# A projection behind attention as two float32r matmuls on split operands, with another order of the first loads and of all steps

## The reference

```
mod = silu(c) @ wmod                      # six rows of 256 per batch: sa, ca, ga, sb, cb, gb
ga, gb = sign * max(|.|, 0.25)
h = layernorm(x) * (1 + ca) + sa
q, k, v = h @ Wq + bq, h @ Wk + bk, h @ Wv + bv      # 16 query heads, 4 key/value heads, 16 wide
q, k = rope(q), rope(k)
att = softmax(causal(q k^T / 4));  y = att v          # per group of 4 query heads, then (B, T, 64)
x = x + ga * (y @ Wo + bo)                            # the projection: 64 -> 256
h = layernorm(x) * (1 + cb) + sb
x = x + gb * ffn(h)       # routed: h + (rmsnorm(h) wv + bv) wo, then a gated block 256 -> 704 -> 256
```

## Time and profile before

| | |
|---|---|
| median of 3 runs | 486.77 us |
| the profiled execution | 489.17 us |
| its span (first to last instruction) | 487.4 us |
| TensorE (PE) busy | 444.7 us |
| VectorE (DVE) busy | 338.9 us |
| ScalarE (ACT) busy | 281.7 us |
| GpSimd (POOL) busy | 225.8 us |
| mean granted TensorE clock | 0.983 of full speed |

### The profile page before, as it was taken

One profiled execution on the slowest core, in us unless ns is written; L12 is line 12 of the kernel. 1 busy time (PEld: TensorE's weight loads), 2 busy tenths in 40 slices (PEclk: granted clock), 3 DMA queues, 4 the chain that ended last, 5 costly groups with the idle time before them and its releaser, 6 DMA issues.

```text
span 487.4 us, 9404 instructions
## 1 busy us (share of the span) xinstructions
PE 444.7 (91%) x3320; PEld 372.3 (76%) x3320; DVE 338.9 (70%) x745; ACT 281.7 (58%) x574; POOL 225.8 (46%) x297
## 2 busy tenths in 40 slices
PE   2687699979999999899999999989999999999994
PEld 2275355677678589778766999879889779999994
DVE  3569968488988337998873688898687635376552
ACT  1183657676559757345487763526857488454440
POOL 5382946621283421331747506275261744348244
PEclk9997989998999999999999999999999999999998
DMA  7904020000000000020020100010001001001011
GB/s 201 300 1 137 2 88 1 1 2 5 3 1 24 1 1 2 1 86 8 3 88 1 34 2 1 5 44 3 1 33 48 1 1 45 1 2 45 1 43 44
DMA packets 16448, 16.04 MB, mean 33 GB/s; under 512 B 4105, under 2 KB 14798, under 8 KB 16402
## 3 DMA queue, kind: packets, MB, share of 16 engines
q1 hardware_dynamic: 16402, 15.43, 10.0%
HBM read 11.09 MB, written 4.21 MB: 31 GB/s over the span
## 4 chain that ended last, share of the span: by engine, by line
PE 80%; DVE 6%; ACT 5%; issue 3%; DMA 2%; SPq 2%; POOL 1%; POOLq 0%; ACTq 0%; DVEq 0%
PE banks L784 8%; PE banks L785 8%; PE banks L786 8%; PE banks L701 8%; PE banks L713 7%; PE banks L675 7%; PE banks L574 5%; PE banks L654 5%; PE banks L575 5%; PE banks L576 5%; PE banks L738 3%; PE banks L664 2%; DMA wm_st<-in_L_wmod 2%; DVE stk L1124 2%; ACT QKT L890 2%
## 5 line engine op out<-in xcount | busy, mean ns | idle before, releaser
L784 PE MATMUL banks<-gTh,guhi 128*128 128x256 f32 x352 | 101.7, 289 | 1.6 <-DVE mx L1139 1.5
L785 PE MATMUL banks<-gTl,guhi 128*128 128x256 f32 x352 | 98.1, 279 | 0.0
L786 PE MATMUL banks<-gTh,gulo 128*128 128x256 f32 x352 | 98.1, 279 | 0.0
L910 ACT ACTIVATE PT<-banks 128x1024 f32<-128x1024 f32 (+3 forms) x96 | 74.4, 809 | 29.0 <-PE banks L701 24.2
L1139 DVE TENSOR_REDUCE mxp<-banks 128x2 f32<-128x1024 f32 (+3 forms) x56 | 62.2, 1142 | 12.1 <-PE banks L675 6.7
L784 PEld LDWEIGHTS banks<-gTh,guhi 128*128 128x128 f32 x352 | 66.5, 189 | 4.2 <-issue 3.5
L785 PEld LDWEIGHTS banks<-gTl,guhi 128*128 128x128 f32 x352 | 66.4, 189 | 0.5
L786 PEld LDWEIGHTS banks<-gTh,gulo 128*128 128x128 f32 x352 | 66.4, 189 | 0.0
L675 PE MATMUL banks<-QKT 128*128 128x512 f32 (+3 forms) x192 | 53.4, 384 | 13.3 <-ACT QKT L890 5.0
L701 PE MATMUL banks<-QKT 128*128 128x512 f32 (+3 forms) x192 | 52.2, 374 | 3.0 <-DMA QKT<-mrT 1.9
L537 POOL TENSOR_SCALAR_AFFINE_SELECT PT<-PT 128x512 f32<-128x512 f32 x32 | 20.7, 647 | 67.6 <-ACT PT L910 67.6
(11 more groups left out here) (165 smaller groups left out, 1069.8 us busy)
## 6 DMA issues: line engine op xcount, KB each, us to landing
xres<-in_L_attn_x SPq DMA_DIRECT2D x8, 512.0 KB, 5.0
out_x<-xres SPq DMA_DIRECT2D x8, 512.0 KB, 3.0
wm_st<-in_L_wmod SPq DMA_DIRECT2D x1, 1024.0 KB, 8.1
modB<-mod_scratch SPq DMA_DIRECT2D x4, 256.0 KB, 3.1
wg_st<-in_L_ffn_w_gate SPq DMA_DIRECT2D x1, 704.0 KB, 5.4
wu_st<-in_L_ffn_w_up SPq DMA_DIRECT2D x1, 704.0 KB, 6.5
xres<-in_L_ffn_w_down SPq DMA_DIRECT2D x1, 640.0 KB, 5.9
wm_st<-in_L_wmod SPq DMA_DIRECT2D x1, 512.0 KB, 4.6
```

Of the source, the lines that this page charges most:

```text
L784: pe.matmul(out_, guhi[:, k, blk, :], gh, start=(m == 0 and k == 0), stop=False)
L785: pe.matmul(out_, guhi[:, k, blk, :], gl, start=False, stop=False)
L786: i = pe.matmul(out_, gulo[:, k, blk, :], gh, start=False, stop=(m == len(blocks) - 1 and k == KB - 1))
L910: act.activation(PT[:, u % 2, 2 * q:2 * q + 2, 0:CH - q0], both("prob", b, n)[:, :, 0:CH - q0], ACT.Exp, scale=float(D) ** -0.5).then_inc( ...
```

## The change

It has three parts.

1. The projection. ytm is now 128 columns wide: a rounded copy of y in the first 64 and the rest (y minus the copy) in the other 64. ynT transposes it to 128 rows; ynev evicts it twice, all 128 rows to yTs and the first 64 to yTo, whose further rows (up to 97) hold ones. A new ScalarE step, woh, rounds Wo_b twice into Wo_h (rows 0 to 63 and 64 to 127) and the bias row once; a new VectorE step, wol, writes the low part of the weight and of the bias into Wo_l. wo is then two float32r matmuls per 128 tokens: yTs by Wo_h (high and low y by the high weight) and yTo by Wo_l (high y by the low weight, and the bias). Wo_raw, Wo_b and mrT share one tile, wo_mr.
2. The first loads. The first half-megabyte of wmod is issued behind the tokens and the weights Wq, Wk and Wv, and not ahead of them. The biases get a semaphore and steps of their own (setb, asetb), so setw and asetw wait for three loads and not for six.
3. ORDER is written anew, with ten more words (setb, asetb, and four each of woh and wol).

```diff
-ACT_STEPS = dict(xev=NJ, sthi=NC, ...
+ACT_STEPS = dict(woh=1, xev=NJ, sthi=NC, ...
-DVE_STEPS = dict(wts=1, wob=1, biasq=1, ...
+DVE_STEPS = dict(wts=1, wob=1, wol=1, biasq=1, ...
 ORDER = """
-ldx ldx pzero stats rstd1 setw stats pmodc pmod vmodc norm1 norm1 rstd1 norm1 asetw vkeys wts xT4 norm1 xT5 pprep0 xev
+ldx ldx pzero stats rstd1 norm1 setw asetw pmodc vmodc wts bias6 norm1 xT4 asetb xev qkv4 setb biasq stats norm1 norm1
...
-        Wo_raw = sb("Wo_raw", [H * D + 1, C])
+        wo_mr = sb("wo_mr", [P, 2, C])
+        Wo_raw, Wo_b = wo_mr[0:H * D + 1, 0, :], wo_mr[0:H * D + 1, 1, :]
+        mrT = wo_mr[P - 32:P - 32 + 2 * H].rearrange("p a c -> p (a c)")
-        Wo_b = sb("Wo_b", [H * D + 1, C])
+        Wo_h = sb("Wo_h", [2 * H * D, C], F32R)
+        Wo_l = sb("Wo_l", [WB, C], F32R)
-        ytm = sb("ytm", [P, TPC, H * D + 1])
-        yT65 = sb("yT65", [H * D + 1, TPC, P])
+        ytm = sb("ytm", [P, TPC, 2 * H * D])
+        yTs = sb("yTs", [2 * H * D, TPC, P], F32R)
+        yTo = sb("yTo", [WB, TPC, P], F32R)
...
-            sp.dma_start(wm_st[:, :, 0:CH], wmod[:, 0:CH].rearrange("(k p) n -> p k n", p=P)).then_inc(l_modc, 16)
             load_x(0, 0)
             sp.dma_start(wq_st[:], Wq.rearrange("(k p) n -> p k n", p=P)).then_inc(l_qkv, 16)
             sp.dma_start(wk_st[:], Wk.rearrange("(k p) n -> p k n", p=P)).then_inc(l_qkv, 16)
             sp.dma_start(wv_st[:], Wv.rearrange("(k p) n -> p k n", p=P)).then_inc(l_qkv, 16)
-            sp.dma_start(bb_st[:, 0:C], bq.partition_broadcast(P)).then_inc(l_qkv, 16)
...
+            sp.dma_start(wm_st[:, :, 0:CH], wmod[:, 0:CH].rearrange("(k p) n -> p k n", p=P)).then_inc(l_modc, 16)
+            sp.dma_start(bb_st[:, 0:C], bq.partition_broadcast(P)).then_inc(l_bias, 16)
...
                 if kind == "ldW":
                     if b > 0:
-                        wait("wo", 0)
+                        wait("wol", 0)
...
                 elif kind == "wo":
                     if n == 0:
-                        wait("wob", 1)
+                        wait("wol", 1)
                     wait("ynev", n * 2 // TPC + 1)
...
                     for t in range(2):
-                        i = pe.matmul(o[:, t * C:(t + 1) * C], yT65[:, (2 * n + t) % TPC, :], Wo_b[:], start=(t == 0),
-                                      stop=(t == 1))
+                        at = (2 * n + t) % TPC
+                        pe.matmul(o[:, t * C:(t + 1) * C], yTs[:, at, :], Wo_h[:], start=(t == 0), stop=False)
+                        i = pe.matmul(o[:, t * C:(t + 1) * C], yTo[:, at, :], Wo_l[:], start=False, stop=(t == 1))
...
+                elif kind == "woh":
+                    wait("wob", 1)
+                    earlier("wo", NJ)
+                    act.activation(Wo_h[0:H * D], Wo_b[0:H * D], ACT.Copy)
+                    act.activation(Wo_h[H * D:2 * H * D], Wo_b[0:H * D], ACT.Copy)
+                    act.activation(Wo_l[WB - 1:WB], Wo_b[H * D:H * D + 1], ACT.Copy).then_inc(S["woh"], 1)
...
-                    act.activation(yT65[:].rearrange("p t n -> p (t n)"),
-                                   of("ynT", b, n)[0:H * D + 1, :], ACT.Copy).then_inc(S["ynev"], 1)
+                    o = of("ynT", b, n)
+                    act.activation(yTs[:].rearrange("p t n -> p (t n)"), o, ACT.Copy)
+                    act.activation(yTo[0:H * D].rearrange("p t n -> p (t n)"), o[0:H * D, :], ACT.Copy
+                                   ).then_inc(S["ynev"], 1)
...
+                elif kind == "wol":
+                    wait("woh", 1)
+                    dve.tensor_tensor(Wo_l[0:H * D], Wo_b[0:H * D], Wo_h[0:H * D].bitcast(F32), ALU.subtract)
+                    dve.tensor_tensor(Wo_l[H * D:H * D + 1], Wo_b[H * D:H * D + 1], Wo_l[WB - 1:WB].bitcast(F32),
+                                      ALU.subtract).then_inc(S["wol"], 1)
...
-                    dve.tensor_tensor(ytm[:, :, 0:H * D].rearrange("p t (h d) -> p t h d", h=H), o[:, :, :, 0:D],
-                                      rc[:].unsqueeze(3).to_broadcast([P, TPC, H, D]), ALU.mult
-                                      ).then_inc(S["ytm"], 1)
+                    hi, y = ytm[:, :, 0:H * D], ytm[:, :, H * D:2 * H * D]
+                    then(dve.tensor_tensor(y.rearrange("p t (h d) -> p t h d", h=H), o[:, :, :, 0:D],
+                                           rc[:].unsqueeze(3).to_broadcast([P, TPC, H, D]), ALU.mult))
+                    then(dve.tensor_copy(hi.bitcast(F32R), y))
+                    dve.tensor_tensor(y, y, hi, ALU.subtract).then_inc(S["ytm"], 1)
```

More of the change, by code:

```diff
@@ L160 @@
-h2lo fft sil ffhi fin a7 up6 a0 rs1 fflo fft ffl route route up1 up4 gate5 gate7 gate0 up6 sil ffhi ms2 fflo fft ms2
-rs2 sil fft down1 sum h2 h2 h2T7 down4 h2hi h2lo sum gate7 gate1 gate4 up5 up3 sil sil ffhi ffhi fflo fft fin ffl ffhi
-sil fflo fft down2 ffhi fft ffhi fflo sum up3 sil fft ffhi fflo down2 ffl down3 down4 sum sum sum fin fin store store
-store
+ldx ldx pzero stats rstd1 norm1 setw asetw pmodc vmodc wts bias6 norm1 xT4 asetb xev qkv4 setb biasq stats norm1 norm1
+xT5 xev qkv5 rstd1 norm1 qkvb qkvb vkeys norm1 xT7 pmod pprep0 norm1 norm1 xT6 xev qkv7 amod afwv pprep1 gmod xev qkv3
@@ new lines @@
+wts up5 sil qkvb qkvb rope gate3 fft ffl fft sthi qkvb stlo qkvb ffhi sil ffhi gate7 h2T5 fflo up4 yT6 h2hi h2lo norm2
+fflo fft sil stack2 up5 stack0 stk max2 up4 ffhi stk fft ytm max6 mxr hT5 hhi ynT2 ynev down0 down1 hmod rs1 ms1 ffhi
+max2 rope mxr sthi hlo max6 gate5 sil sum sum max0 mxr stlo mxr stack2 stk max6 max2 fin wo5 mxr mxr ffl fft mxr max6
+max0 max2 mxr mxr max6 max0 up4 fflo mneg mxr mxr ffhi fflo x1 mtT2 mrow gate3 sil fft stack6 rs1 stk down3 mxr sum
+max4 gate2 max6 sil rstd2 up3 max0 ffhi ffl store mrd mxr wo4 woh ldx mxr mxr max6 mxr fft x1 prob0 max6 mxr prob2 exp
@@ new lines @@
+up2 mxr ms1 rs1 max0 gate5 sil mxr route mxr ms2 ffhi rstd2 max6 mxr a3 hhi route fft stack0 stk hlo fflo ms2 up7 up3
+max0 mxr max4 mxr gate6 sil wo2 ffhi woh gate0 x1 fft max4 rs2 h2 ffhi sil h2 down6 down7 fflo mxr fft h2T1 h2hi ffhi
+sum max4 stack2 a6 sum norm2 fflo mxr ffl down7 h2lo mneg fin route ldG down0 max4 sum sum stk a3 max0 hmod hT2 ms2
+mtT7 mxr route mrow mrd store ms2 ms1 rs2 gate5 max6 sil rstd2 up3 max4 mxr mxr h2 h2 gate6 h2T7 h2hi max0 fft mxr
+norm2 ffhi hhi h2lo hlo prob4 up3 gate7 gate2 sil fft fin rs1 ffhi sil hmod ms1 mxr wol sil rs1 ffl exp up3 fflo fft
```

158 lines of the change are left out of this document (79 added, 79 removed).

## The result

The changed kernel took 485.09 us (median, 482.81 to 487.75), the kernel before 487.69 us on the same chip (484.96 to 490.08): ratio 0.9944, 95% interval [0.9928, 0.996]. It is 0.56% faster, some 2.7 us, where 1.6% was forecast. The sign was right and the size wrong: 0.9944 of the 486.77 us of the prediction is 484.0 us, 4.9 above the forecast and beyond its own range of 476 to 482 (the wider range, 472.5 to 485.5, takes in the rivals and holds it). The profiled run took 484.3 us.

A forecast was written before the change was run, and what follows sets the result against it. TensorE was taken to bound the kernel behind 64 us, a chain of loads, vector work and maxima ahead of it. 489.17 - 5.8 - 2.5 + 0.6 = 481.5 us profiled, median 479.1; own range 476 to 482, wider 472.5 to 485.5.

The forecast's parts named there:

- The projection's passes: Projection on TensorE: 64 float32 passes of 0.216 us become float32r at 0.113; 5.8 us less, bounds 3.3 to 6.6.
- The added work elsewhere: Added VectorE and ScalarE instructions for splits, copies and evictions, mostly hidden behind TensorE: +0.6 us, bounds 0 and +10.1.
- The head: Ahead of 64 us: new loads' order and earlier copy of the maxima rows; -2.5 us, bounds 0 and -4.5.
- The copy of the maxima rows: Head, ScalarE: mrow moves ahead of two weight pieces and the down weight, so the first prob gains 1.5 us.
- The loads' order: Head: first half-megabyte of modulation weight goes behind tokens and three projection weights; 1.0 us gained.
- the landing and the 23.6 us behind it: Head: modulation weight in at 8.9 us; first stack starts 23.6 us later, at 32.5 to 34.3 us.
- The rest of the order: Nearly every engine's row changes place; taken as worth nothing, since order does not tell how long it waits.
- the limit of 13.8 us: TensorE's empty time between 64 and 480 us, the most that an order can win there.
- Order gives back: Rival: the 5.8 us turn into new waits where VectorE is nearly full; 484 us, chance 0.16.
- Better packing: Rival: the order also closes part of TensorE's 13.8 us of gaps, say 6 us more; 473 us, chance 0.14.
- The weight load rules: Rival: each float32r pass is held to its 0.189 us weight load, 1.7 us instead of 5.8; 483 us, chance 0.04.
- Slower by VectorE: Rival: 24 added VectorE instructions are paid, with blocks by GpSimd; 488.6 up to 504, value 490 us, chance 0.11.

The follow-up runs named there:

- the run in the old order: Kernel before, its loads and order kept, with the new projection alone put in, the weight's split right behind its product with the modulation: ratio 1.0244, 12 us slower.
- the mark: The changed kernel once more, unaltered, run beside three kernels with shifted operand places: ratio 0.994 [0.9923, 0.9957] to the kernel before.

## Why the prediction was right in sign and wrong in size

*The projection's passes* (5.8 us forecast, 4.5 measured, give or take 1.6). The mechanism was right: 64 float32r records for 64 float32 passes, and the size is within the noise. The distance of starts was mis-sized, 0.120 us where 0.113 was taken from the down product of the earlier trace rows, which is 0.4 us in all. The operands' distance does not explain it: it was 64 in the earlier trace rows and is 64 here, and 192 in its place left 0.120 as it was. Why the projection's starts lie 0.120 us apart stays open. The Trainium skill (Perfetto Trace Analysis, "Identifying the Most-Contended Engine") judges TensorE's headroom by the share of peak arithmetic and by the weight loads' busy share. The rival drawn from the second, that nothing is won where no load goes away, was not borne out: 64 loads remain (6.1 us on each line), and the passes won 4.5 us.

*Nothing else on TensorE changes its speed.* This was never written as a step, it was assumed in the sum, and **it is the largest miss**: the earlier trace rows was read as a property of float32r. It is one of float32r and two addresses. Moving the feed-forward operands from distance 192 to 160 (gate, up) and from 64 to 96 (down) cost 2.3 us (0.994 against 0.9892, give or take 1.4; 2.0 us between the two runs on one chip). The trace of after showed it as 281 ns in the place of 279 on an untouched line, and as a busy sum that fell by 2.7 us instead of 6 or more.

*The added work elsewhere* (0.6 forecast, 2.3 measured, give or take 2.3; bounds 0 to 10.1). The rows are as sized: VectorE rose by 12.0 us, 10 forecast, ScalarE by 10.1, 9 forecast. The step that failed, as far as the noise lets it be told, is taking the low end "because TensorE, not VectorE, ends the waits": in the chain VectorE's share went from 6% to 11%, and the new projection brought 2.4 us of idle time in the profiles. That the new order hides most of the added work fits all runs. How much of it the matmuls ahead of the projection hide is not shown, since the run in the old order lost much of its time at the split of the weight, which the forecast priced at 0.1 us.

*The head* (2.5 forecast). The copy of the maxima rows: 1.5 forecast, 1.8 by itself. The loads' order: the landing and the 23.6 us behind it came out to within 0.3 us. Both are partly luck. The landing lies anywhere from 8.4 to 10.2 us in the ten profiles, and in the sum behind it two errors cancel: the first qkv took 2.90 us where 1.5 was put down and the bias product 1.65 instead of 0.7, while pmod took 3.60 instead of 5.85. The stack did start 2.0 us earlier than before, and yet the sign of the term was wrong, since I compared it with the old program and not with the new program and the old loads; in the new order of work the early weight is used at once, and the new place costs 1.5 to 2.2 us. That the first prob came 4 us earlier than forecast shows in little: most of the head's empty time came back between 64 and 130 us.

*The rest of the order* (0 forecast). Order and loads with the old projection are worth 3.1 us; less the copy's 1.8 and with the loads' 1.5 to 2.2 taken out, some 3 us are the rest of the order, good to no better than 2 us. Nothing in the profile before told these 3 us, and the limit of 13.8 us holds.

With measured terms: -4.5 (passes) + 2.3 (added work) + 2.3 (distance) - 3.1 (order and loads) = -3.0 us. This is no check. The added work is itself the passes less the ratio of two other runs, and in the sum every run but the mark cancels, so it returns the mark's own 0.994, 2.9 us. What the terms do show is where the 5.0 us between forecast and measurement lie: 1.3 in the passes, 2.3 in the addresses, 1.7 in the added work, and 0.6 the other way in order and loads, each good to between 1.2 and 2.3 us.

*The rivals.* "Order gives back" had the right size of time and the wrong cause: the order gave, and the addresses, the added work and the loads took. "Better packing" came by some 3 us of its 6. "The weight load rules" named 483 us, but its sign, a distance of 0.19 us, did not come. "Slower by VectorE" did not come either; the run in the old order shows VectorE as the one that TensorE waits for, though there it is VectorE that waits for ScalarE.

## What to carry to other kernels

When a change adds or resizes a tile in SBUF, compare the mean duration and the distance of starts of matmuls that it did not touch: float32r products can change speed by some per cent with the distance between their operands' addresses, and a few unused bytes put that right. Look at where each new step stands in the row of its engine: a split whose second half waits for another engine cost VectorE 6.2 us of waits in one order and none in the other. Test order and arithmetic apart, since here each of them alone tells a different story (12 us slower, 0.6% faster). A load moved back in the queue is free only if nothing in the new program could have used it earlier.

## What the runs showed of the hardware

- The distance of starts of 128x128 by 128x256 float32r matmuls runs from 113.3 to 121.6 ns with the two operands' addresses alone, no other engine at work; float32 (215.8 ns for each of a product's two records) and bfloat16 (109.2 ns) don't move. The Trainium skill (SBUF — State Buffer, "Who interferes with whom") says that only the port pair of VectorE and GpSimd causes contention; that is a rule on two engines at once. Here TensorE runs alone and still depends on where its two operands lie, which the rule does not cover. What in the memory does it, no run here shows.
- Eight qkv matmuls took 2.90 us at 16.12 us and 1.54 us at 20.44 us in the changed kernel, and the eight of the modulation product 5.85 us before and 3.60 after the earlier trace rows, while the granted clock of these stretches is listed as 1.00. The trace's records of the clock begin only at 19.3 us in the changed kernel and at 20.7 us before; what lies ahead of the first record is listed as 1.00. In all twelve traces with the new order of work these eight matmuls took 2.90 us ahead of the first record and 1.46 to 1.54 behind it, wherever it stood (18.6 to 26.4 us). So the times point to the lower level of the clock in that stretch, and its end differs by up to 8 us from run to run.
